# Second attention: who normalises an image, and who makes the high halves of the values

## The reference, cut to what matters

```python
h = h + _L1_attn_ref(_layernorm(h, axis=-1), L1_attn_W_qkv, L1_attn_W_0)

def _layernorm(x, axis=-1, eps=1e-05):
    m = jnp.mean(x, axis=axis, keepdims=True)
    v = jnp.var(x, axis=axis, keepdims=True)
    return (x - m) / jnp.sqrt(v + eps)

qkv = x @ W_qkv                      # 12 heads of 64
s = jnp.einsum('ghid,ghjd->ghij', q, k) * scale
a = jax.nn.softmax(s, axis=-1)
out = jnp.einsum('ghij,ghjd->ghid', a, v)   # then @ W_0
```

## Time and profile before

| | before |
|---|---|
| runs, median | 2405.19 us |
| the profiled execution | 2403.57 us, of which the span from first to last instruction 2401.8 us |
| PE busy | 90% of the span |
| PE weight loads | 71% |
| DVE busy | 82% |
| ACT busy | 85% |
| POOL busy | 70% |
| granted TensorE clock, mean | 0.988 of full speed |

### The profile page before, as it was taken

The page is one execution under the profiler, slowest core; times in us unless marked ns, Lnnn a source line. Parts: engine busy times, 40 slices in busy tenths (PEclk is TensorE's granted clock), DMA queues, the critical chain, the costliest instruction groups (busy, mean ns, idle before and its releaser), DMA issues. The chain is left out here.

```text
span 2401.8 us, 76354 instructions
## 1 busy us (share of the span) xinstructions
PE 2168.1 (90%) x25422; PEld 1700.2 (71%) x25422; DVE 1979.7 (82%) x4966; ACT 2034.0 (85%) x5745; POOL 1672.2 (70%) x2165
## 2 busy tenths in 40 slices
PE   5899999999999799999999999999999999988876
PEld 5788885888878577777777777777777777765554
DVE  5666776888787689899989989999899999976875
ACT  4677776777776599999999999999999999996997
POOL 5667761333332488989899999989899999992323
PEclk9899999999999999999999999999999999999999
DMA  6334420000100276666666666666666666671111
GB/s 189 92 110 120 120 71 28 6 5 5 44 15 5 35 122 125 119 123 121 120 121 121 122 119 126 119 121 120 124 120 124 121 121 119 122 119 40 53 51 54
DMA packets 734155, 222.64 MB, mean 93 GB/s; under 512 B 667590, under 2 KB 732720, under 8 KB 733808
## 3 DMA queue, kind: packets, MB, share of 16 engines
q1 hardware_dynamic: 734064, 221.56, 45.0%
HBM read 46.49 MB, written 9.68 MB: 23 GB/s over the span
## 5 line engine op out<-in xcount | busy, mean ns | idle before, releaser
L1516 POOL TENSOR_TENSOR b_pr<-b_pr,fc 128x394 f32<-128x394 f32 (+1 forms) x768 | 651.5, 868 | 122.2 <-DVE fc L1436 122.2
L1365 ACT ACTIVATE b_pr<-b_scores,fc 128x197 f32<-128x197 f32 (+1 forms) x1536 | 630.2, 437 | 2.4 <-issue 1.2
L1501 POOL TENSOR_TENSOR b_halves<-b_pr,b_halves 128x394 f16<-128x394 f32 (+1 forms) x640 | 564.8, 908 | 31.0 <-ACT b_halves L1334 27.0
L1273 PE MATMUL b_banks<-fp,wqkv 128*128 128x197 f16 x3840 | 377.5, 249 | 42.7 <-DVE b_qk L1420 38.6
L1430 DVE TENSOR_REDUCE fc<-b_scores 128x2 f32<-128x394 f32 x768 | 395.9, 557 | 4.0 <-PE b_scores L1291 1.9
L1273 PEld LDWEIGHTS b_banks<-fp,wqkv 128*128 128x128 f16 x3840 | 319.7, 98 | 83.9 <-DVE b_qk L1420 60.5
L1334 ACT ACTIVATE b_halves<-b_pr 128x788 f16<-128x788 f32 x384 | 341.3, 889 | 4.7 <-POOL b_pr L1516 4.7
L1365 ACT ACTIVATION_READ_ACCUMULATOR b_pr<-b_scores,fc 128x1 f32 (+1 forms) x1536 | 337.5, 220 | 0.0
L977 POOL TENSOR_TENSOR h<-h,fp_bias 69x192 f32 (+3 forms) x128 | 133.4, 1070 | 266.8 <-DVE m_xn L139 266.8
L1420 DVE SCALAR_TENSOR_TENSOR b_qk<-b_banks,b_qk 128x394 f16<-128x394 f32 x384 | 215.0, 560 | 99.9 <-ACT b_qk L1348 99.7
L1280 PE MATMUL b_banks<-wqkv,fp 128*128 128x384 f16 (+1 forms) x1280 | 254.6, 330 | 40.4 <-DVE h L1455 38.8
(11 more groups left out here) (251 smaller groups left out, 4387.2 us busy)
## 6 DMA issues: line engine op xcount, KB each, us to landing
patches<-in_x SPq DMA_DIRECT2D x64, 588.0 KB, 4.3
b_pt<-b_halves SPq DMA_TRANSPOSE x384, 3.2
out<-z_res SPq DMA_DIRECT2D x64, 96.0 KB
fc<-b_halves SPq DMA_TRANSPOSE x192, 3.2
fp<-b_halves SPq DMA_TRANSPOSE x192, 3.2
m_raw_weights<-in_wqkv SPq DMA_DIRECT2D x2, 1152.0 KB, 6.9
out<-z_res SPq DMA_DIRECT2D x32, 51.8 KB
h<-h SPq DMA_DIRECT2D x32, 44.2 KB
```

The lines of the kernel that those rows point to most:

```text
L1273: last = t.matmul(out[:, g * SEQ:(g + 1) * SEQ], w[:, (2 * n + g) * P:(2 * n + g + 1) * P], x, start=(j == 0), stop=(j == 4))
L1365: last = nc.scalar.activation(pr[n % 3][0:ROWS[c], c, e, :], scores[n % 2][0:ROWS[c], e, c * SEQ:(c + 1) * SEQ], ACT.Exp, bias=nmx[n % 2][ ...
L1501: nc.gpsimd.tensor_tensor(halves[n % 3][0:ROWS[c], c, 1, :, 0:SEQ], pr[n % 3][0:ROWS[c], c], halves[n % 3][0:ROWS[c], c, 0, :, 0:SEQ], ALU ...
L1516: last = nc.gpsimd.tensor_tensor(p, p, inv, ALU.mult)
```

## The change

ACT takes over n: four activations `Identity` with a bias (minus mean times reciprocal deviation, in `shift`, made once at the start by DVE) and a scale. DVE takes over three of the four high parts of the values, as steps u1, u2 and u3; v0 stays on ACT. The semaphore for the high parts is split in two, by engine. All four orders are rewritten: among others, PE does w after s0 and directly before x' (before: between v2 and q5, with q5, s0 and v3 ahead of x'), ACT puts q5 and h3 between e4 and e5, h4 before x, and n between o1 and e3; POOL takes p and l by turns. POOL has the same five low parts as before, and DVE keeps l4.

```diff
-    PE_ORDER = ("v0 m4^^ s4^ v1 q4 m5^^ s5^ v2 w^^ q5 s0 v3 x' m0^ m1^ s1 q0' q1' "
-                "m2^ s2 q2' q3' s3 m3^").split()
-    ACT_ORDER = ("o1^ v0' e3 v1' h1 q4' o2^ h2 v2' e4 e5 q5' h3 v3' x'' h4 o0 e0' h5 "
-                 "q0'' q1'' e1' h0' q2'' e2' q3''").split()
-    DVE_ORDER = ("m5^ v2 n' r4^ w^^ r5^ q5 m0 v3 x' l4^ r0 m1 q0' o0^ q1' m2 r1 q2' "
-                 "m3 q3' o1^ v0' r2 m4 r3 v1' q4' o2^").split()
-    POOL_ORDER = ("p3^ p4^ l3^ p5^ k^^ p0 l5^ l0 p1 p2 l1 l2").split()
+    PE_ORDER = ("m3^^ q3 v1 s4^ m4^^ q4 m5^^ v2 s5^ q5 v3 s0 w^^ x' m0^ s1 m1^ q0' "
+                "q1' s2 m2^ v0' q2' s3").split()
+    ACT_ORDER = ("q4' o2^ h2 e4 q5' h3 e5 h4 x'' e0' o0 h5 q0'' q1'' e1' h0' v0'' "
+                 "q2'' e2' h1' q3'' o1 n''' e3'").split()
+    DVE_ORDER = ("q5 u3 v3 m0 r5^ w^^ x' l4^ r0 m1 q0' q1' r1 o0^ m2 v0' q2' m3 r2 "
+                 "q3' u1' o1^ v1' m4 r3 q4' u2' o2^ v2' m5 r4").split()
+    POOL_ORDER = ("p0^ l5^^ p1^ l0^ p2^ l1^ p3^ k^^ l2^ p4^ l3^ p5^").split()
...
+        V_ON_VECTOR = sorted(number(s) for s in DVE_ORDER if s[0] == "u")
+        V_ON_SCALAR = [n for n in range(4) if n not in V_ON_VECTOR]
...
+                    if kind == "n":
+                        if later(img):
+                            act.wait_ge(x_ready, img)
+                        elif img == 0:
+                            act.wait_ge(filled, 1)
+                        for c in range(2):
+                            rows, j = slice(0, ROWS[c]), bass.ds(2 * img + c, 1)
+                            move, scale = S["shift"][rows, j], S["rstd"][rows, j]
+                            twice = h[rows, img, c, P:D].unsqueeze(1).to_broadcast([ROWS[c], 2, LO])
+                            nc.scalar.activation(xn[rows, c, 0:P], h[rows, img, c, 0:P], ACT.Identity, bias=move, scale=scale)
+                            last = nc.scalar.activation(xn[rows, c, P:2 * P].rearrange("p (a b) -> p a b", a=2), twice, ACT.Identity, bias=move, scale=scale)
+                        last.then_inc(xn_made, 1)
...
                 for r in range(2):
-                    last = v.memset(rsum[r][:], 1.0)
-                last.then_inc(filled, 1)
+                    v.memset(rsum[r][:], 1.0)
+                v.scalar_tensor_tensor(out=S["shift"][:], in0=S["mean"][:], scalar=-1.0, in1=S["rstd"][:], op0=ALU.mult, op1=ALU.mult).then_inc(filled, 1)
...
-                    if kind == "n":
-                        if later(img):
-                            dve.wait_ge(x_ready, img)
-                        for c in range(2):
-                            last = normalise_twice(nc.vector, S, xn[0:ROWS[c], c], 2 * img + c, ROWS[c], img, c)
-                        last.then_inc(xn_made, 1)
+                    if kind == "u":
+                        dve.wait_ge(v_ready, 4 * img + n + 1)
+                        if n % 2 == 0 and later(PAIRS * (img - 2) + 3):
+                            dve.wait_ge(mixed, PAIRS * (img - 2) + 3 * (n // 2) + 3)
+                        c, col, at = n % 2, (n // 2) * VH, job_bank("v", n)
+                        v.tensor_copy(val[odd][0:ROWS[c], 0, c, col:col + VH], banks[0:ROWS[c], at, 0:VH]).then_inc(high_by_v, 1)
```

More of the change, by code:

```diff
@@ L1161, in attention_1 @@
         freed = [sem(f"b_freed{c}") for c in range(2)]
-        (xn_made, xt_hi, xt_split, qk_hi, qk_split, v_hi, v_split, inverted, prob_made,
+        (xn_made, xt_hi, xt_split, qk_hi, qk_split, v_split, inverted, prob_made,
          high_made, mixed, ot_hi, ot_split, filled, cleared, x_ready, q_ready, v_ready, w_ready, h_updated) = map(sem, (
-             "b_xn_made", "b_xt_hi", "b_xt_split", "b_qk_hi", "b_qk_split", "b_v_hi", "b_v_split",
+             "b_xn_made", "b_xt_hi", "b_xt_split", "b_qk_hi", "b_qk_split", "b_v_split",
              "b_inverted", "b_prob_made", "b_high_made", "b_mixed", "b_ot_hi",
              "b_ot_split", "b_filled", "b_cleared", "b_x_ready", "b_q_ready", "b_v_ready", "b_w_ready", "b_h_updated"))
+        high_by_s, high_by_v = sem("b_high_by_s"), sem("b_high_by_v")
+        V_ON_VECTOR = sorted(number(s) for s in DVE_ORDER if s[0] == "u")
+        V_ON_SCALAR = [n for n in range(4) if n not in V_ON_VECTOR]
         LOW_ON_POOL = sorted(number(s) for s in POOL_ORDER if s[0] == "l")
@@ L1189, in low_made, with v_high @@
             return signal, 2 * len(by) * (img + before) + 2 * by.index(n) + c + 1
+        def v_high(img, n):
+            signal, by = (high_by_v, V_ON_VECTOR) if n in V_ON_VECTOR else (high_by_s, V_ON_SCALAR)
+            return signal, len(by) * img + by.index(n) + 1
         def turned(img, n):
@@ L1339, in step @@
                         act.wait_ge(*made(s, img))
-                    if kind == "x":
+                    if kind == "n":
[10 more added lines that the diff above has]
+                        last.then_inc(xn_made, 1)
+                    elif kind == "x":
                         if later(img):
@@ L1353, in step @@
                         c, col = n % 2, (n // 2) * VH
-                        copy(val[odd][0:ROWS[c], 0, c, col:col + VH], banks[0:ROWS[c], k, 0:VH]).then_inc(v_hi, 1)
+                        copy(val[odd][0:ROWS[c], 0, c, col:col + VH], banks[0:ROWS[c], k, 0:VH]).then_inc(high_by_s, 1)
                     elif kind == "e":
@@ L1422, in step @@
                     elif kind == "v":
-                        dve.wait_ge(v_hi, 4 * img + n + 1)
+                        dve.wait_ge(*v_high(img, n))
                         c, col = n % 2, (n // 2) * VH
```

## The result

| | before | after |
|---|---|---|
| runs, median (5 each, on one chip) | 2405.19 us (2402.74 to 2406.37) | 2392.36 us (2389.25 to 2394.82) |
| ratio | | 0.9946, interval 0.9932 to 0.9960 |
| the profiled execution | 2403.57 us, span 2401.8 | 2392.77 us, span 2390.9 |
| granted TensorE clock, mean | 0.988 | 0.986 |

The changed kernel is faster by 0.54%. The forecast was 2386 us, its range 2364 to 2412. One run of E1 took 3468.87 us at a granted clock of 0.557 and is left out of its median.

The account below looks back on a forecast made before the run. ACT was taken as the fullest engine, delayed by DVE's normalising; afterwards ring W (odd, 21.24 us) and ring P (even, 20.25) set rounds. 2403.57 - 22 + 3 + 1 = 2385.6, 2387 against the median; said 2386, range 2364 to 2412.

Parts of the forecast that it names:

- The rings: Two dependency loops longer than ACT's work, sharing ACT's stretch e0 to e3 (12.87 us); the longer sets each round.
- e0: ACT's step of exponentials after x; needs l3's buffer, 0.08 us later; forecast to wait for POOL's low part in even rounds.
- Rival C: Ring W shorter than walked, so ring P sets both rounds (20.25 and 20.87 us): 2371 us; chance 0.15.
- ring P: From e3 through POOL's p3, k (odd only), l2, p4, l3 to e0: even rounds 20.25 us, odd 20.87.
- The price of n: Four normalising activations on ACT at 0.39 us each, 1.57 together, between 1.3 and 2.25 us a round.
- rival B: n on ACT costs 0.56 instead of 0.39 us an instruction, so slower: 2423 us; chance 0.18.
- rival E: `Identity` makes ACT reload its tables between exponentials, adding 164 us; chance 0.02.
- The price of u: Each copy of 384 columns out of PSUM on DVE: 0.42 us (0.30 to 0.57), three times 1.3 us.
- Ring W: From e3 through ACT's q5, DVE's low part, PE's w and transposes to ACT's x: odd rounds 21.24 us, even 19.78.
- Rival D: l4 on DVE delays m1 and so e1; odd rounds lose some 0.5 us: 2400 us; chance 0.20.
- The sum: Whole time: 22 us less over 61 rounds, 3 us back for small gaps, 1 us for the stage's start.
- rival A: The forecast itself: both rings as walked, rounds 20.25 and 21.24 us with gaps up to 0.15: 2380 to 2396; chance 0.45.

Follow-up runs that it names:

- E2: Changed kernel with half of PE's products of w left out in odd rounds; 2350.55 us, one run.
- E1: Changed kernel with DVE's written order cut elsewhere, so the loop's turn falls between m4 and r3 instead of before q5; 2389.29 us, ratio 0.9950.
- E11: Changed kernel with half of POOL's p4 ahead of the even x left out (one of two multiplies); 2386.19 us, one run.
- E3: Changed kernel with two of the four normalising activations n on ACT left out from the second image on; 2344.04 us, one run.
- E9: Changed kernel with half of POOL's p4 left out, meant for even rounds but falling into odd ones; 2392.41 us, one run.
- E5: Changed kernel with the three high parts u1, u2, u3 moved from DVE back to ACT, n staying on ACT; 2444.18 us, one run.
- E6: Changed kernel with w's two statistics instructions on DVE moved behind q1; 2388.27 us, ratio 0.9929.
- E12: Changed kernel with earlier loop turn and statistics behind q1 on DVE, plus a third of PE's m1 ahead of odd q0 left out; 2374.92 us, one run.
- E4: Kernel before with only n moved from DVE to ACT, high parts of the values still on ACT; 2461.11 us, ratio 1.0250.

## Why the prediction was right, and where it was off

**The rings.** Right: x waits in odd rounds for PE with w just before, e0 in even rounds for POOL's l3, and each answers to its own cut (E2, E11), while n answers in both (E3). Rival C, ring P in both rounds, is excluded: the odd rounds keep 21.9 us when p4 shrinks (E9), and fall to 20.6 when w does (E2).

**The price of n.** 1.57 us forecast, 1.54 measured: the nearer row (0.44 with 192 columns) was the right one to take, and rival B is out. A single instruction lasts 0.53 us and not the 0.45 to 0.50 that were said; what counts is the distance between two starts. The Trainium skill, ScalarE: Activation LUTs, What ACT_TABLE_LOAD costs, makes 386 ns of such an instruction, an estimate from its figures that the distance of 0.385 us bears out. No table load stands among ACT's groups from 1300 to 1900 us, and in the whole trace there are as many as before (rival E).

**The price of u.** 0.42 us was taken, 0.57 was the upper bound. These are groups of DVE from 1300 to 1900 us:

```profile
L1433 DVE CAST b_val<-b_banks 69x384 f16<-69x384 f32 x57 | 31.0, 544 | 0.0
...
L1433 DVE CAST b_val<-b_banks 128x384 f16<-128x384 f32 x29 | 15.9, 548 | 0.0
```

It was 0.54. The row that was taken for the middle value, 256 columns in 0.295 us, reads f16, and these copies read f32. What left ACT counts for 1.65 of 2.22 us in two rounds (E5). That what comes to DVE costs nothing fits the rows, where none of ACT's waits stands behind a u, but no run tests it alone.

**Ring P, the even round.** 20.25 forecast, 20.09 measured. The term q4 to e0 was 7.38 and is 7.24: I added up durations of POOL's instructions, but neighbours overlap (1.60 and 1.73 from start to start for 1.64 and 1.77). In odd rounds, where E2 shows the ring, k was too long as well (0.62 for 0.28).

**Ring W, the odd round: the step that failed.** 21.24 forecast, 21.92 measured, 0.68 more. The hand-over between q5's high and low part was read off as 0.04; there it stands in the middle of DVE's order, but in the new order it is the first step, behind the loop's turn. With 0.08 at w's start and 0.03 for the high part's duration that is the 0.31 from q5 to x. The other 0.36 are q1. The prediction took it for covered, with a margin of 0.1 us, and it had less than nothing: w's statistics on DVE (E6) and m1 on PE (E12) stood in front of it, 0.2 and 0.16 us. So the 3 us set aside for gaps should have been 16: (0.68 - 0.16) x 30.5.

**Rival D.** l4 on DVE takes 1.05 us in odd and 1.75 in even rounds, and POOL's p0 stands 2.01 us idle behind it. But ACT shows no wait at e1 or h1 in the groups, and when POOL stands idle there for 2.80 us (E9) no round moves. So it is no cause, as far as the rows say; no run shortens l4 itself.

**The sum.** The forecast counted -22, +3 and +1. Measured in the two profiles: -8.1 in the 61 rounds, +1.0 in the two rounds before them (34.66 to 35.70 us), +0.8 before the first x (8.86 to 9.68), -0.9 behind the last, and -3.8 ahead of the stage: together 10.9, the difference of the spans. The 3.8 aren't the change's: the first row of L137 comes at 399.4 us before and 395.6 after, and among the profiles of E1 to E12 between 393.6 and 399.6. So the change's own stage gives some 7 us where 18 were forecast, less than half. The medians say 12.8, with an interval from 10 to 16; where the rest of these is could not be found, since only one profile of before shows its stages. That the time came to lie inside rival A's 2380 to 2396 is therefore in part luck: with the stage's 7 us alone the median would have been about 2398, still inside the whole range of 2364 to 2412. The mechanism was right, and its gain was put too high.

**What was not forecast at all** is how dear n is by itself. The prediction put ACT's own sum 1.7 us below the round; E4 shows that moving n gives back only some 0.6 us of this. By the Trainium skill, ScalarE: Activation LUTs, Rules for kernel authors, an addition and multiplication belong on VectorE. E4 alone (+59 us) agrees with that; the whole change, 13 us faster, does not, since three copies went the other way in it. By the rows of single instructions the trace does not agree either: beside POOL three of n's four took 0.88 us on DVE, and on ACT each costs 0.385.

## What to carry to other kernels

In this kernel, work that moved to the fullest engine paid only because other work left it in the same change: n cost 59 us alone, and the copies that left gave back 54. When orders are written by hand, look at what the first step of a loop's order is, and keep what nobody waits for (statistics) behind what somebody waits for. And in a software pipeline with two kinds of rounds, measure a round from a place that both critical rings share; a distance between two marks on one of the rings puts a wait into the wrong round, as it did in the expectation of E6.

## What the runs showed of the hardware

- A loop's turn on DVE delayed the instruction behind it by 0.2 us: 0.24 us from ACT's end to DVE's start in the kernel with the turn there, 0.04 in E1. In even rounds of the changed kernel, where the body has no turn, it is 0.03:

```profile
1521.51 0.57 DVE L1440 SCALAR_TENSOR_TENSOR b_qk<-b_banks,b_qk 128x394 f16<-128x394 f32 x1
```

  (ACT's high part ended at 1521.48.)
- A copy of 384 columns out of PSUM, f32 to f16, takes 0.54 us on DVE, nearly what the two-input low part does (0.55). The 256 columns of the earlier trace rows take 0.295, but from f16 and on 64 partitions; which of these differences counts is not shown.
- On ACT, an activation with bias and scale from memory costs 0.385 us from start to start for 128 columns, no more than a plain copy of 394 columns out of PSUM (0.38).
